# Two graph layers on one core: node updates and the second layer's tables moved into the edge loops, one program per engine

## What is computed

```python
# layer 0, batch = 0 for all nodes
msg  = relu(concat([x[dst], x[src], edge_attr, u[0]]) @ W1.T + b1)
agg  = segment_sum(msg, dst, 6250)
y    = relu(concat([x, agg, u[0]]) @ W2.T + b2)
x    = layernorm(x + y)
# layer 1
h    = relu(concat([x[src], x[dst], edge_attr]) @ msg_w1 + msg_b1)
m    = h @ msg_w2 + msg_b2
agg  = segment_sum(m, dst, 6250) / max(count, 1)      # 0 where count is 0
y    = relu(concat([x, agg]) @ upd_w1 + upd_b1) @ upd_w2 + upd_b2
x    = layernorm(x + y)
```

## Time and profile before

| | us |
|---|---|
| median of 3 runs | 4139.44 |
| lowest, highest | 4138.32, 4142.05 |
| the profiled execution | 4140.49 |
| its span, first to last instruction | 4138.7 |

### The profile page before, as it was taken

The page is one execution under the profiler, slowest core; times in us unless marked ns, Lnnn a source line. Parts: engine busy times, 40 slices in busy tenths (PEclk is TensorE's granted clock), DMA queues, the critical chain, the costliest instruction groups (busy, mean ns, idle before and its releaser), DMA issues. The chain is left out here.

```text
span 4138.7 us, 53825 instructions
## 1 busy us (share of the span) xinstructions
PE 3378.5 (82%) x16906; PEld 3171.1 (77%) x16906; DVE 1671.5 (40%) x3965; ACT 591.0 (14%) x1005; POOL 2981.5 (72%) x3156
## 2 busy tenths in 40 slices
PE   6998788877888888788779878878788787887886
PEld 4998787777878778787759877777777777777773
DVE  4544444444444444444445443434333333333333
ACT  1111111111111111111321111111111111111113
POOL 4777777777777777777267777777777777777772
PEclk6555555555555555555755555555555555555556
DMA  6554444444444444444155444444444444444431
GB/s 227 167 162 130 140 131 145 143 133 140 131 140 142 139 140 131 140 135 143 53 159 172 140 142 140 131 139 130 140 143 138 140 131 140 132 148 141 131 118 34
DMA packets 286577, 569.11 MB, mean 138 GB/s; under 512 B 165416, under 2 KB 197523, under 8 KB 248976
## 3 DMA queue, kind: packets, MB, share of 16 engines
q1 hardware_dynamic: 185326, 357.82, 25.7%
q0 software_dynamic: 100096, 205.20, 18.6%
q10 hardware_dynamic: 866, 2.56, 0.2%
HBM read 545.86 MB, written 19.45 MB: 137 GB/s over the span
## 5 line engine op out<-in xcount | busy, mean ns | idle before, releaser
L206 POOL DMA_INDIRECT Qr<-tabQ,srcE x3128 | 2960.7, 947 | 1074.7 <-issue 969.1
L615 PE MATMUL bank<-wall,BIG 128*128 128x128 f32 x6256 | 1596.3, 436 | 35.0 <-DMA BIG<-in_eaT 35.0
L628 PE MATMUL bank<-BIG 128*128 128x42 f32 x6256 | 1459.8, 413 | 13.0 <-ACT BIG L557 13.0
L615 PEld LDWEIGHTS bank<-wall,BIG 128*128 128x128 f32 x6256 | 1419.2, 331 | 35.4 <-DMA BIG<-in_eaT 35.4
L628 PEld LDWEIGHTS bank<-BIG 128*128 128x128 f32 x6256 | 1420.7, 331 | 13.6 <-ACT BIG L557 13.6
L587 DVE TENSOR_TENSOR BIG<-bank,Qr 128x512 f32<-128x512 f32 x782 | 539.6, 690 | 2097.9 <-issue 1727.3
L619 PE MATMUL bank<-BIG 126*128 126x128 bf16 x3128 | 484.1, 310 | 648.4 <-DVE BIG L570 647.8
L557 ACT ACTIVATE BIG<-BIG 128x512 f32<-128x512 f32 x782 | 492.4, 630 | 3364.1 <-DVE BIG L587 3364.1
L619 PEld LDWEIGHTS bank<-BIG 126*128 126x128 bf16 x3128 | 339.3, 141 | 774.8 <-DVE BIG L570 748.1
L570 DVE TENSOR_TENSOR BIG<-bank,BIG 126x512 bf16<-126x512 f32 x782 | 534.2, 683 | 34.3 <-DMA BIG<-in_dstR 34.0
L576 DVE TENSOR_TENSOR BIG<-bank,relE 128x168 f32<-128x168 f32 x782 | 251.5, 322 | 0.0
(11 more groups left out here) (94 smaller groups left out, 481.0 us busy)
## 6 DMA issues: line engine op xcount, KB each, us to landing
BIG<-in_eaT SPq DMA_DIRECT2D x196, 1024.0 KB, 5.6
BIG<-in_dstR SPq DMA_DIRECT2D x96, 1008.0 KB
Qr<-tabQ,srcE POOLq DMA_INDIRECT x3128, 2.5
BIG<-tabP SPq DMA_DIRECT2D x782, 31.5 KB
tabP<-BIG SPq DMA_DIRECT2D x24, 384.0 KB, 2.8
tabQ<-BIG SPq DMA_DIRECT2D x24, 256.0 KB, 4.0
X<-in_xN SPq DMA_DIRECT2D x1, 3136.0 KB, 12.0
out<-BIG SPq DMA_DIRECT2D x12, 256.0 KB, 2.3
```

The costliest lines, as they stand in the source:

```text
L206: e.indirect_dma_start(Q[:, g % R_Q, j, :], None, tabQ[l][:, :], bass.IndirectOffsetOnAxis(ap=srcE[:, g, j:j + 1], axis=0)).then_inc(es[l] ...
L615: e.matmul(bank[i % R_C][:, j * D:(j + 1) * D], ea[:, k % R_EA, (i % LQ * J + j) * P:(i % LQ * J + j + 1) * P], wc[l], start=(j == 0), sto ...
L628: last = e.matmul(bank[4 + g % 2][:, 0:W], M[:, g % R_M, j, :], S[:, g % R_S, j, :], start=(j == 0), stop=(j == J - 1))
```

## The change

The work of `update(0)`, of `between` and of `update(1)` is cut into 13 units (`UN`: eleven of four blocks, one of two, one of three) and done inside the edge loops. A table `READY` gives for each unit the number of groups after which its nodes get no more edges, by the square-root law plus two groups; three steps later (`DUE`) the unit starts, and its parts follow on the engines at fixed distances in steps. The check of the edge list is extended (`lim`) to test that table against the actual edges; where it fails, the old phases run instead. After the first block there is one block for all the rest: each engine goes from layer 0 into layer 1 in its own time, held by semaphores alone. GpSimd waits for the 13 stores of the new `tabQ` and then starts layer 1's gathers. The indicator moves from POOL to DVE, the stores of the tables and the output from SP to ACT. The clearing of `AC` is done unit by unit.

To make room, the rings shrink: `R_Q` 12 to 10, `R_S` 6 to 4, `R_C` 4 to 3 (bank 3 and bank 7 serve the units), and `bc` is loaded four groups at a time instead of eight. The last group gathers 3 tiles instead of 4, since only 320 of its edges are real.

```diff
-R_EA, R_PB, R_BC, R_Q, R_ST, R_S, R_M, R_PT = 2, 4, 2, 12, 3, 6, 3, 4
-LB = 8
-R_C = 4
-PF = R_Q - 2
+R_EA, R_PB, R_BC, R_Q, R_ST, R_S, R_M, R_PT, R_U = 2, 4, 2, 10, 3, 4, 3, 4, 2
+R_C = 3
+PF = R_Q
...
+UN = [(b, 4) for b in range(0, 44, 4)] + [(44, 2), (46, NB - 46)]
+READY = [min(NG, math.ceil(NG * math.sqrt(min(N, (b + n) * P) / N)) + 2) for b, n in UN[:-1]] + [NG]
+DUE = [g + 3 for g in READY]
+def due(i, lag):
+    return DUE.index(i - lag) if i - lag in DUE else None
...
         def gathers(e, l, g0, g1):
             for g in range(g0, g1):
-                if g >= R_Q:
-                    e.wait_ge(es[l]["tt"], g - R_Q + 1)
-                for j in range(J):
+                i = l * NG + g
+                if i >= R_Q:
+                    e.wait_ge(fs["tt"], i - R_Q + 1)
+                for j in range(tiles(g)):
...
+                e.wait_ge(s_lim, NU)
+                link(e.tensor_tensor(lim[:, :], lim[:, :], baseI[:, 0:NG], ALU.subtract))
+                link(e.tensor_reduce(stat[0:1, 4:5], lim[:, :], AX, ALU.max))
+                e.tensor_scalar(vio[:, 4:5], stat[:, 4:5], 0.0, None, ALU.is_gt)
...
-                for at3, n3, fr in ((0, 4, crow[0:1, 2:3, :].broadcast_to([1, 4, D])), (4, 1, bank[7][0:1, 2 * D:3 * D].unsqueeze(1))):
+                for k, (at3, n3, fr) in enumerate(((0, 4, crow[0:1, 2:3, :].broadcast_to([1, 4, D])), (4, 1, bank[7][0:1, 2 * D:3 * D].unsqueeze(1)),
+                                                   (5, 4, rows[0:1, 2:3, :].broadcast_to([1, 4, D])))):
...
+        def fast_gpsimd(e):
+            gathers(e, 0, PF, NG)
+            units_stored(e, s_tabQ[1])
+            gathers(e, 1, 0, NG)
...
+            for l in range(2):
+                for g in range(LAST + 6):
...
+                    if l == 0:
+                        if (u := due(g, 5)) is not None:
+                            q1(u)
+                        if (u := due(g, 3)) is not None:
+                            x1t(u)
+                        if (u := due(g, 0)) is not None:
+                            y0(u)
+                    else:
+                        if (u := due(g, 3)) is not None:
+                            y1(u)
+                        if (u := due(g, 1)) is not None:
+                            hidden(u)
```

More of the change, by code:

```diff
@@ L1 @@
+import math
 import concourse.bass as bass
@@ L288, in _ @@
                                 pattern=[[-3, W - 1]], channel_multiplier=1).then_inc(s_cst, 1)
+                e.memset(lim[:, 0:READY[0]], 0.0).then_inc(s_lim, 1)
+                for u in range(NU - 1):
+                    e.memset(lim[:, READY[u]:READY[u + 1]], float((UN[u][0] + UN[u][1]) * P)).then_inc(s_lim, 1)
                 e.wait_ge(s_src, 16)
@@ L636, in build @@
-        edges(0)
         at = 0
@@ new lines, in update_scalar, with relu, root, norm @@
+        def update_scalar(e, l):
+            x = us[l]
+            x_y, x_var, x_sd, x_nm, x_n, x_t, x_tc, x_q, x_qv, x_o = (x[n] for n in ("y", "var", "sd", "nm", "n", "t", "tc", "q", "qv", "o"))
+            x_u = x_q
+            def relu(c):
+                w, h = CH[c][1] * P, c % 2
+                e.wait_ge(x_u, c + 1)
+                if c >= 2:
+                    e.wait_ge(x_y, c - 1)
+                e.activation(uT[:, h, 0:w], bank[4 + h][:, 0:w], ACT.Relu, bias=ub1c).then_inc(x_qv, 1)
+            def root(c):
+                n, h = CH[c][1], c % 3
+                e.wait_ge(x_var, c + 1)
+                e.activation(rs[:, h, 0:n], rs[:, h, 0:n], ACT.Sqrt).then_inc(x_sd, 1)
+            def norm(c):
+                b, n = CH[c]
+                h = c % 3
+                e.wait_ge(x_nm, c + 1)
+                if l == 1 and c >= 2:
+                    e.wait_ge(x_o[c % 2], 16 * (c // 2))
+                to = X[:, b:b + n, :] if l == 0 else O[:, c % 2, 0:n, :]
+                for k in range(n):
+                    last = e.activation(to[:, k, :], Y[:, h, k, :], ACT.Identity, bias=nm[:, h, k:k + 1], scale=sd[:, h, k:k + 1])
+                last.then_inc(x_n, 1)
+            def xt_copy(c):
+                b, n = CH[c]
+                e.wait_ge(x_t, c + 1)
+                e.copy(XT[:, b * P:(b + n) * P], bank[2 + c % 2][:, 0:n * P]).then_inc(x_tc, 1)
+            def q_copy(c):
+                n = CH[c][1]
+                e.wait_ge(x_q, c + 1)
+                if c >= R_PT:
+                    e.wait_ge(s_tabQ[1][c % R_PT], 16 * (c // R_PT))
+                e.copy(PT[:, c % R_PT, 0:n * D], bank[4 + c % 2][:, 0:n * D]).then_inc(x_qv, 1)
+            if l == 0:
+                steps((0, root), (1, norm), (2, xt_copy), (3, q_copy))
+            else:
+                steps((0, relu), (1, root), (2, norm))
@@ new lines, in meet @@
+        def meet(e, k):
+            e.drain()
+            e.sem_inc(s_meet, 1)
+            e.wait_ge(s_meet, 5 * k)
+        p1s = [p1[n] for n in ("c", "hi", "r", "mid", "lo")]
+        at = 0
+        f_eaT, at = carve(at, [R_EA, LQ * GE])
+        M, at = carve(at, [R_M, J, D])
+        S, at = carve(at, [R_S, J, W])
+        S16, at = carve(at, [R_S, W], BF16)
+        ST, at = carve(at, [R_ST, GE], BF16)
+        bc, at = carve(at, [R_BC, LQ * GE], I16)
+        PB, at = carve(at, [R_PB, D], BF16)
```

874 lines of the change are left out of this document (546 added, 328 removed).

## The result

| | before | after |
|---|---|---|
| median of four runs, us | 4139.81 (4138.32 to 4142.05) | 4006.34 (4004.98 to 4006.63) |
| profiled execution, us | 4140.49 | 4006.16 |
| its span, us | 4138.7 | 4004.4 |
| mean granted clock of TensorE | 0.517 | 0.553 |

A forecast was written before the change was run, and what follows sets the result against it. The prediction took POOL's chain of gathers, 1.25 us each, plus the places where POOL stands still, as the bound. Its terms summed to -125.8 us from a span of 4138.7, giving 4012.9, a forecast time of 4014 us (4000 to 4036).

The forecast's parts named there:

- start, to the 49th gather: Start of layer 0: longer first block and ring of 10 delay POOL's gathers, +12.7 us (+8 to +18).
- gathers: Both edge loops: one tile fewer to gather in each layer, 1.25 us each, -2.5 us.
- seam: Between the layers: last to next gather takes 21.5 us (18 to 30) instead of 72.78, -51.3 us.
- layer 1's second stop: Early layer 1: POOL's 8.33 us wait for the end of between becomes the normal 0.31, -8.0 us.
- VectorE against gathers: Layer 1's loop: mean, with two SBUF inputs, stretches twelve gathers by 0.41 us each, +4.9 us (0 to +15).
- tail: Last gather to end of span: 20.0 us (18 to 26) instead of 101.56, -81.6 us.
- Units inside the loops, 0 on the path: Both edge loops: ring of 10 groups and TensorE's spare 0.97 us per group hide the units, 0 us.
- TensorE at 1.2 GHz: Unit work: matmuls priced at this clock, 9.9 us per four-block unit in layer 0, some 6.7 in layer 1.
- TensorE's total busy time unchanged within 3%: Sign expected in the profile after, whole program: TensorE equally busy within 3%, its share up.
- The first rival: Edge loops: new memsets, indicator and small products on DVE delay 26 more gathers by 0.41 us, 4025 us; chance 0.13.
- TensorE as the bound: Edge loops: work moved in is only moved, +203 us against -125.8, 4217 us, slower; chance 0.03.
- the seam keeping half its length: Between the layers: last unit or its store comes late, seam 45 us instead of 21.5, 4037 us; chance 0.06.

The follow-up runs named there:

- the doubled products: Changed kernel with the edge-feature products of every group made twice: 4011.12 us, ratio 0.9677 to the kernel before.
- the memset: Changed kernel with one unused 1024-wide VectorE memset added after every fourth group: 4006.43 us, ratio 0.968 to the kernel before.
- added tensor_scalar: Changed kernel with one unused 1024-wide VectorE tensor_scalar on an SBUF operand added after every fourth group: 4029.29 us, ratio 0.9737 to the kernel before.
- ring of 6: Changed kernel with the ring Q of 6 groups instead of 10, the first block issuing 6: 4026.6 us, ratio 0.973 to the kernel before.
- three products per unit: Changed kernel with the products of y0 issued three times in layer 0's units 0 to 11: 4006.52 us, ratio 0.9681 to the kernel before.
- the new order: Changed kernel with ring Q of 13 groups and, in last_terms, X's addition ahead of the counts' clamping: 3998.35 us, on another chip 3992.79 us.

## Why the prediction was right, and where it was off

The forecast of 4014 (4000 to 4036) was 7.7 us above the 4006.34 measured. The mechanism held: POOL's chain of gathers is the time, and the gain lies in the seam and the tail. About half of the 7.7 us is luck, the gathers' own period; the rest is in the sizes of the terms. Term by term, from the two profiled executions:

| term | predicted | measured | from |
|---|---|---|---|
| start, to the 49th gather | +12.7 | +13.6 | 108.47 + 8 x 1.248 - 104.86 |
| gathers | -2.5 | -2.5 | one less in each layer |
| seam | -51.3 | -52.7 | 20.11 - 72.78 |
| layer 1's second stop | -8.0 | -8.9 | with a 0.9 us wait soon after it |
| VectorE against gathers | +4.9 | +2.6 | 6.7 us in 18, before 4.1 in 10 |
| gathers' own period | 0 | -4.1 | below |
| tail | -81.6 | -82.3 | 19.28 - 101.56 |
| sum | -125.8 | -134.3 | 4004.4 - 4138.7 |

*Start.* Right in kind and size, and moved by the size of the ring as reckoned. One microsecond was missing. TensorE began at 104.22, 7.0 us after the issue of the edge features at 97.26, where the prediction's 98.28 + 4.4 gives 102.7: 1.5 us later. The smaller `bc` saved more than the 1.8 us reckoned, 2.3, since VectorE began 1.27 after TensorE instead of 3.60.

*Seam and tail.* The chain of the last unit went as written down. The 7.3 us from the last gather to complete sums, which the prediction said would stay, were 6.5 and 6.1: VectorE's last addition of gathered rows began 2.34 and 2.44 us after the last gather's start, where it was 3.55 and 3.59. The last gather is now one of 64 rows instead of 128; whether that is the reason was not tried. The rest of the seam was 13.6 for 14.2: the store took 2.3, not 3.3. In the tail the six last products took 0.94 us at the upper clock, for which the prediction had 1.45, and the output's last DMA was issued 14.8 us after the last gather instead of 17.2. Against this, the end of the span came 4.5 us after that issue, not 2.9. What is left of the two is the 0.7 us of the table.

*Units inside the loops, 0 on the path.* Right: POOL's row is the same in the earlier trace rows and in the change. There was more room than was argued, and of another kind. The prediction counted 0.97 us per group to spare on TensorE at 1.2 GHz; the doubled products put 2.06 us, reckoned at that clock, on each group without a cost, because the clock rose.

*TensorE's total busy time unchanged within 3%.* Wrong: 3378.5 to 3188.6, 5.6% less. The step that failed is "TensorE at 1.2 GHz" for the whole loop; part of the time it now runs at 2.4.

*VectorE against gathers.* The mechanism is right and the term mis-sized. `mean` was to stretch 12 gathers by 0.41; it stretched 6, by 0.1 to 0.4, since it stands behind the sums and falls at no fixed place against the gathers. `last_terms` stretched 12 where it was 10. The first rival, in which the new memsets and small products also held gathers, is refuted: the memset cost nothing, and instructions with a PSUM input held none. The added tensor_scalar did hold gathers, so the rival's instruction can do it, but in the change's trace all 18 stretched gathers stand beside `last_terms`' addition or `mean`, and none beside the indicator.

*The period of the gathers.* Half of the miss. Away from stretched gathers it was 1.2497 us in the profiled execution of before and 1.2483 in the change's, over some 3,080 gathers 4.1 us. This is not seen to come from the change, and its cause is open: the profiled executions with the ring of 6 and with three products per unit show 1.2495 and 1.2496, the new order's first one 1.2503, all others 1.2482 to 1.2483, with the same instructions on POOL. The execution with 1.2496 took 4009.67, and the other three of that kernel 4005.7 to 4006.7; with the doubled products the profiled execution, at 1.2482, took 4004.98, and the other three on the same chip 4009.8 to 4012.6.

*The other rivals.* TensorE as the bound (4217) and the seam keeping half its length (4037) did not come about: the first is refuted by the doubled products, the second by the seam's rows. The Trainium skill (Perfetto Trace Analysis, Identifying the Most-Contended Engine) would have named TensorE by its weight loads, which lead still, 75% to 74%; the runs speak against it here.

## What to carry to other kernels

An engine that shows 74% can be full: add what its sequencer takes between instructions (here 0.31 us on each gather of 0.94) before calling anything else the bound, and test it by giving the busier engine more work. Work that follows a loop can go inside it, unit by unit, as soon as its inputs are final; under this chain of gathers it cost nothing measurable. What then remains is the last unit's chain of small steps and what the rings hold at the start. Beside a chain of indirect DMAs on GpSimd, keep VectorE's additions and products of two SBUF operands off the moment at which a gather starts (with one of the two inputs in PSUM none held a gather), and its tensor_scalars on SBUF from running over either end of one.

## What the runs showed of the hardware that was not expected

- The granted clock of TensorE was higher where more was put into the loops: 0.50 before, 0.53 to 0.57 with the units, 0.59 in layer 0 with three first products, 0.83 to 0.84 with 36 to 40% more matmuls. The busy share hardly moved with it, and fell in the last, so at the lower clock it was no measure of the room left. The number of matmuls alone does not set the clock: layer 1's stretch has 7317 before and after, at 0.50 and 0.53.
- An addition with both inputs in SBUF that runs over a gather's start holds it for its whole rest less 0.13 us (0.52 us on average in 183 cases), and one that starts inside the gather did not hold it (153 cases). A tensor_scalar started 0.17 to 0.52 us into a gather held it to 0.12 us behind its own end (25 cases); started 0.55 to 0.75 us in, it was held itself.
- The mean period of the gathers in a profiled execution was one of a few values, 1.2483, 1.2496 or 1.2503 us, from one execution or chip to another, for the same kernel too (1.2503 and 1.2483 with the new order, on two chips). Over 3,100 gathers these are 4 to 6 us, as much as the smaller effects here, which is why the last 3.6 us were compared on one chip.
